# Four graph layers on one core: the first weights' product in column halves, and the last layer's third T inside the first maximum's turn

## What is computed

```
h = jnp.maximum(_layernorm(x, axis=-1), 0.0)          # layer 0
q = h @ Wq.T + bq;  k = h @ Wk.T + bk;  v = h @ Wv.T + bv
a = q @ k.T / sqrt(256) + adj + adj
x = x + softmax(a, axis=-1) @ v
...
h = jnp.maximum(_layernorm(x, axis=-1), 0.0)          # layer 3
g = h @ W
scores = where(adj + eye > 0, g @ U @ g.T, -inf)
att = softmax(scores, axis=-1)
x = x + (S * att) @ g                                 # S = adj + eye
```

## Time and profile before

| | |
|---|---|
| median of 3 runs | 401.05 us (400.98 to 401.45) |
| profiled execution | 400.99 us, its span 399.2 us |
| PE busy | 386.3 us, 97% of the span |
| DVE busy | 338.0 us, 85% |
| ACT busy | 251.9 us, 63% |
| POOL busy | 119.3 us, 30% |

### The profile page before, as it was taken

The page is one execution under the profiler, slowest core; times in us unless marked ns, Lnnn a source line. Parts: engine busy times, 40 slices in busy tenths (PEclk is TensorE's granted clock), DMA queues, the critical chain, the costliest instruction groups (busy, mean ns, idle before and its releaser), DMA issues. The chain is left out here.

```text
span 399.2 us, 7765 instructions
## 1 busy us (share of the span) xinstructions
PE 386.3 (97%) x2651; PEld 355.7 (89%) x2651; DVE 338.0 (85%) x772; ACT 251.9 (63%) x529; POOL 119.3 (30%) x131
## 2 busy tenths in 40 slices
PE   8999999999999999999999999999999899999894
PEld 6788888999899899999999889998988688989794
DVE  5898899899994857999999989766887988799894
ACT  2454699888785658785787992245242466257772
POOL 1290000000010424223041011051010499469982
PEclk9999999999999999999999999999999999999988
DMA  7995000000000001000000000000000000010011
GB/s 241 377 380 167 0 0 2 2 0 2 0 2 0 2 0 54 2 2 0 3 2 0 3 0 2 0 2 2 0 2 0 0 2 2 0 54 1 2 53 36
DMA packets 10318, 13.98 MB, mean 35 GB/s; under 512 B 660, under 2 KB 7208, under 8 KB 10280
## 3 DMA queue, kind: packets, MB, share of 16 engines
q1 hardware_dynamic: 9736, 12.96, 9.5%
q10 hardware_dynamic: 544, 0.52, 0.4%
HBM read 12.10 MB, written 1.39 MB: 34 GB/s over the span
## 5 line engine op out<-in xcount | busy, mean ns | idle before, releaser
L1611 PE MATMUL ps<-v_hi,p_hi 128*128 128x258 f32 (+3 forms) x242 | 64.0, 295 | 0.4 <-DVE x_sb L998 0.2
L397 POOL TENSOR_TENSOR mr_all<-mr_all,mhalf 128x4 f32<-128x4 f32 (+1 forms) x12 | 13.1, 1088 | 165.0 <-DVE mr_all L894 165.0
L1612 PE MATMUL ps<-v_lo,p_hi 128*128 128x258 f32 (+3 forms) x242 | 60.9, 281 | 0.0
L1611 PEld LDWEIGHTS ps<-v_hi,p_hi 128*128 128x128 f32 (+3 forms) x242 | 44.6, 184 | 2.2 <-issue 0.9
L1612 PEld LDWEIGHTS ps<-v_lo,p_hi 128*128 128x128 f32 (+3 forms) x242 | 44.7, 185 | 0.6
L1616 PE MATMUL ps<-v_hi,p_lo 128*128 128x258 f32 (+3 forms) x242 | 40.1, 284 | 1.1 <-DVE p_lo L1178 1.1
L980 DVE TENSOR_TENSOR s_sb<-s_sb,ps 128x512 f32<-128x512 f32 (+3 forms) x63 | 38.4, 611 | 0.8 <-PE ps L1598 0.7
L434 POOL TENSOR_TENSOR mid_lo<-adjT_sb,mid_hi 128x512 fp32r<-128x512 f32 (+2 forms) x16 | 20.9, 1306 | 49.7 <-ACT mid_hi L669 49.7
L1616 PEld LDWEIGHTS ps<-v_hi,p_lo 128*128 128x128 f32 (+3 forms) x242 | 32.5, 185 | 1.6 <-DVE p_lo L1178 1.6
L1903 PE MATMUL ps<-big_hi,p_lo 128*128 128x256 f32 (+3 forms) x121 | 32.7, 299 | 0.6 <-ACT p_lo L854 0.5
L1611 PE MATMUL ps<-big_hi,mid_hi 128*128 128x258 f32 (+3 forms) x121 | 31.8, 294 | 0.0
(11 more groups left out here) (251 smaller groups left out, 1218.3 us busy)
## 6 DMA issues: line engine op xcount, KB each, us to landing
adjT_sb<-in_adjT_dram SPq DMA_DIRECT2D x1, 2816.0 KB, 16.5
adjT_sb<-in_adjT_dram SPq DMA_DIRECT2D x3, 768.0 KB, 8.9
adjT_sb<-in_adjT_dram SPq DMA_DIRECT2D x1, 1815.0 KB, 20.9
out_dram<-x_sb SPq DMA_DIRECT2D x10, 128.0 KB
x_sb<-in_x_dram SPq DMA_DIRECT2D x2, 256.0 KB, 3.8
x_sb<-in_x_dram SPq DMA_DIRECT2D x1, 512.0 KB, 3.9
adjT_sb<-in_adjT_dram SPq DMA_DIRECT2D x1, 512.0 KB, 11.1
rows_sb<-in_rows_dram SPq DMA_DIRECT2D x1, 385.0 KB, 11.2
```

The costliest lines, as they stand in the source:

```text
L1611: pe.matmul(out_ap, left_[0][0:k, n % RING, mine], right_[0][0:k, j, 0:cols_], start=(j == 0), stop=False)
L1612: pe.matmul(out_ap, left_[0][0:k, n % RING, mine], right_[1][0:k, j, 0:cols_], start=False, stop=False)
```

## The change

**Beginning.** The product of the weights is made in column halves: `weight_half(m)` gives columns m*128 to m*128 + 127 of both row blocks, so that part m of T needs half m alone (before, a half was one row block, and each part needed both). Half 1 has a 129th column: ACT copies bk behind Wk (`wk_sb` is 257 wide now), and the product with Wq comes out with the half; the eight passes of `weight_column(6, ...)` go, and PE waits for that copy (`col_set`). z is (x + (-mean)) times the root, so for the first group POOL's second operation goes. One `idle` matmul is added ahead of the product, the one ahead of `weight_column(6, ...)` goes. `values(0)` stands ahead of the first score, `values(1)` between the score's halves. ACT and DVE follow that order; DVE splits `wb` and does the second group's statistics ahead of T's split, and `bqc` moves behind them.

**Layer 3.** `make_t(2, 1)` moves from step 9 to step 11, between `turn_max(0)` and `spread_max(0)`; `values(8)` goes behind `spread_max(0)`. On DVE the split of that T goes behind `shift(0)`, and the zeroing of `spare_mask` takes its old place at step 9. T's third group lies in banks 0 and 3 in place of 6 and 7; on ACT the first `w_hi` goes ahead of `values(10)` and waits for T's split.

```
-B0 = Banks([0, 1], [2, 3], [3, 7], [6, 5], [4, 5, 6, 7])
+B0 = Banks([0, 1], [2, 3], [7, 3], [6, 5], [4, 5, 6, 7])
-T3_BANKS = [[0, 1], [6, 7], [6, 7]]
+T3_BANKS = [[0, 1], [6, 7], [0, 3]]
...
+                if layer == gi == 0:
+                    ins.then_inc(ln, 1)
+                    return
...
-            for m in range(C):
-                act.wait_ge(gq_mm, m + 1)
-                split(0, wa_hi[:, m, 0:D], ps[:, 7 - 4 * m, m * D:(m + 1) * D], HALF_SCALE)
+            act.wait_ge(cols_in, 16)
+            act.activation(wk_sb[:, :, D:D + 1], bk_col.unsqueeze(2), ACT.Copy).then_inc(col_set, 1)
+            act.wait_ge(gq_mm, 1)
+            split(0, wa_hi[:, :, 0:P], half_product(0)[:, :, 0:P], HALF_SCALE)
             for b in range(4):
                 h_hi(b, 0)
+            act.wait_ge(gq_mm, 2)
+            act.activation(raw_b[:, :, D:D + 1], half_product(1)[:, :, P:P + 1], ACT.Copy, scale=HALF_SCALE).then_inc(col_set, 1)
+            split(0, wa_hi[:, :, P:D], half_product(1)[:, :, 0:P], HALF_SCALE)
...
+            t_hi_part(2, 1)
             values(8, 1)
-            for n in range(NT):
+            exp3(0)
+            values(9, 1)
+            exp3(1)
+            act.wait_ge(t_lo[1], 2 * NG)
+            w_hi(0)
+            values(10, 1)
+            for n in range(2, NT):
                 exp3(n)
-                if n < 2:
-                    values(n + 9, 1)
-                if n:
-                    w_hi(n - 1)
+                w_hi(n - 1)
...
-            dve.wait_ge(gq_mm, 1)
-            split_lo(0, wa_lo[:, 0, 0:D], ps[:, 7, 0:D], wa_hi[:, 0, 0:D], HALF_SCALE, 1)
             dve.wait_ge(ln, 1)
             for b in range(4):
-                dve.tensor_scalar(z_buf[:, b, :], x_sb[:, b, :], mr_all[:, b, 1:2], mr_all[:, b, 0:1], ALU.mult,
-                                  ALU.add).then_inc(zd, 1)
-            split_lo(0, wa_lo[:, 1, 0:D], ps[:, 3, D:2 * D], wa_hi[:, 1, 0:D], HALF_SCALE, 2)
+                dve.tensor_scalar(z_buf[:, b, :], x_sb[:, b, :], mr_all[:, b, 0:1], mr_all[:, b, 1:2], ALU.add,
+                                  ALU.mult).then_inc(zd, 1)
+            split_lo(0, wa_lo[:, :, 0:P], half_product(0)[:, :, 0:P], wa_hi[:, :, 0:P], HALF_SCALE, 1)
             for b in range(4):
                 h_lo(b, 0)
+            split_lo(0, wa_lo[:, :, P:D], half_product(1)[:, :, 0:P], wa_hi[:, :, P:D], HALF_SCALE, 2)
...
+            def weight_half(m):
+                n = P + m
+                for k in range(C):
+                    for c in range(C):
+                        ins = pe.matmul(half_product(m)[:, k, 0:n], wq_sb[:, c, k * P:(k + 1) * P], wk_sb[:, c, m * P:m * P + n],
+                                        start=(c == 0), stop=(c == C - 1))
+                ins.then_inc(gq_mm, 1)
...
                 for c in range(C):
+                    if a == 0 and n == 0 and c:
+                        values(1, 0)
                     pe.wait_ge(t_lo[a], 2 * gi + c + 1)
...
-                if s == 9:
-                    make_t(2, 1)
-                if s == 11:
-                    pe.wait_ge(t_lo[1], 2 * NG)
-                    turn_max(0, 1)
+                if s == 11:
+                    pe.wait_ge(t_lo[1], 2 * C)
+                    turn_max(0, 1)
+                    make_t(2, 1)
+                    spread_max(0, 1)
                     values(8, 1)
-                    spread_max(0, 1)
```

More of the change, by code:

```diff
@@ L901, in h_lo, with t_lo_part @@
                                          op1=ALU.subtract).then_inc(hlo, 1)
-            def t_lo_part(gi, a):
-                for m, bank in enumerate(T3_BANKS[gi] if a else B0.moved):
+            def t_lo_part(gi, a, parts=(0, 1)):
+                for m in parts:
+                    bank = (T3_BANKS[gi] if a else B0.moved)[m]
                     at_ = slice(gi * BANK, gi * BANK + CW[gi])
@@ L1501, in turn, with weight_product @@
                 ins.then_inc(zt, 1)
-            def weight_product(bank, lhsT, rhs, halves=range(C)):
-                for m in halves:
+            def weight_product(bank, lhsT, rhs):
+                for m in range(C):
                     for c in range(C):
@@ L1543, in values, with make_t @@
                 project(ps[0:rows(b), bank, 0:n], b, layer, (wb_hi, wb_lo), n).then_inc(v_mm[a], 1)
-            def make_t(gi, a):
+            def make_t(gi, a, parts=range(C)):
                 layer = 3 if a else 0
@@ L1554, in make_t @@
                 hT = hT3 if a else hT0
-                for m, bank in enumerate(T3_BANKS[gi] if a else B0.moved):
+                for m in parts:
+                    bank = (T3_BANKS[gi] if a else B0.moved)[m]
+                    if a == gi == 0:
+                        pe.wait_ge(wlo[0], m + 1)
                     wait(pe, t_lo[a], 2 * (gi - 1) + m + 1)
@@ L1661, in _ @@
                 score(s, 0)
-                if s == 0:
-                    pe.wait_ge(wlo[1], 1)
-                    pe.wait_ge(col_set, 1)
-                values(s, 0)
+                if s == 1:
+                    pe.wait_ge(col_set, 4)
+                if s > 1:
+                    values(s, 0)
                 if s == 6:
```

65 lines of the change are left out of this document (33 added, 32 removed).

## The result

The changed kernel takes 398.62 us (median of 9 runs, 398.40 to 399.11) where the kernel before takes 401.05 (9 runs, 400.73 to 404.35): a ratio of 0.9936 with a 95% interval of 0.9918 to 0.9954. It is faster by 2.43 us. The prediction had the sign, but its 399.9 and its range (399.1 to 401.1) lie above the result: the gain is more than twice the 1.1 us forecast. The profiled execution took 398.4 us, its span 396.6.

What follows compares the result with a forecast made beforehand. PE was taken to bound the steady part, with time to gain only at its waits and idle passes: 400.99 less 0.65 (beginning) and 0.45 (layer 3) gives 399.9 us. Own range 399.4 to 400.4, full range 399.1 to 401.1.

Steps and rivals of the forecast that it cites:

- z starts near 7.75: Beginning: with POOL's multiplication and DVE's split out of its way, z starts 0.8 us earlier than 8.54.
- The passes of 128 columns: Weights' product at the beginning: passes 0.12 us apart, like the turn's, so half 0 takes 1.0 us.
- The rival of halves as dear as before: Beginning: a 128-column pass costs what one of 256 does, the beginning gives 0.1, 400.4 to 400.5; chance 0.12.
- DVE's chain to T's split "is what is last": Beginning: DVE's chain, not PE, is last; T's split starts near 14.8, 0.55 us later than before, the score at 15.7.
- PE's own arrival: Beginning: PE reaches the first half of the score at 15.5 and waits 0.2 us there for DVE.
- From there on nothing waits: Beginning, from the score's first half: `values(1)` between the halves covers the second split (0.75); both are done at 18.0.
- The prediction's bound of 1.0: Beginning: upper bound of its gain, 1.0 us if PE meets no wait at all; 0.65 was taken.
- Layer 3: Late place of the change: T's 1.84 us on PE hide the reduction, first `shift` 0.9 earlier, first sum 0.45 earlier.
- The bound of 0.65: Layer 3: upper bound of its gain, 0.65 us if DVE's split overlaps better; 0.45 was taken.
- A fall of the clock at the beginning: Rival on the clock at the beginning, chance 0.10; part of it, 0.07, is slower than 401.85.
- DVE stays behind: Rival: DVE's room runs out; the beginning gives only 0.3 or layer 3 only 0.15, time 400.2; chance 0.12.
- more than forecast: Rival: nothing waits in either place, the beginning or layer 3, time 399.2; chance 0.08.

Runs made afterwards that it cites:

- the late zeroing: Changed kernel with DVE's zeroing of `spare_mask` moved from step 9 to behind the last operation of the running extreme: 398.39 us, then 398.16 against the changed kernel's 398.61.

## Why the prediction was wrong

- **z starts near 7.75**: 7.57, right; x had landed 0.16 earlier, by chance. The weights' product started at 6.64 and not at 7.05, as the clock had risen earlier, at 6.0; behind z that changed nothing. The passes of 128 columns: 9.28 to 10.17 for eight, 0.11 apart, right. The rival of halves as dear as before is refuted.
- **DVE's chain to T's split "is what is last", the step that failed.** The working put half 1 at 9.6 to 10.55, ACT's copy and split of it at 10.8 to 11.4, `wb_hi` to 12.05, the statistics at 12.7 and T's split at 14.8. Measured: half 1 at 9.28, `wb_hi` from 10.71 to 11.35, the statistics at 11.99, T's split at 13.92, 0.88 earlier, and what is last is PE. Of half 1's 0.3, z's own start is 0.18. ACT adds 0.4: the copy, the split and `wb_hi` start 0.07 and 0.27 apart, 0.34 in all, where the working had 0.6, near the sum of the durations (0.17 + 0.38), and the hand-over from half 1 was 0.1 shorter. The working took starts for DVE and durations for ACT. ACT's three operations in a row overlap by 0.10 and 0.11 us here (10.37 + 0.17 against 10.44, 10.44 + 0.38 against 10.71), and that alone is half of the 0.4. From the statistics on the working was nearly right, 1.93 against 2.1.
- **PE's own arrival, which then decided,** was costed at 15.5 and was 15.01: T started at 10.99 and not 11.4, for half 1's 0.3 and 0.1 less for half 1 and the bias column. So the 0.87 by which the turn of block 4 came before 18.0 is made of three parts: 0.2 that DVE's chain was not last (15.7 against PE's 15.5), 0.5 of PE's own arrival, and 0.18 behind it, 2.12 against 2.3, since half a score takes 0.70 and not 0.8. DVE's chain costed right would have given 17.8 and not 17.13: each term on PE was a little too dear as well.
- **"From there on nothing waits"** and the swap of `values` were right, and are worth 1.0 of the 1.5. The prediction's bound of 1.0, PE meeting no wait, was too low since it counted the waits and not what stood before them.
- **A term that was missing**: 0.57 between the places, 0.3 of it at 99 us. Some 0.4 is there in every trace and goes with the number of DVE's instructions; the rest is this pair of executions. Nothing in the diff tells it, but the wait put down to "issue" stood in the trace of before.
- **Layer 3**: the turn comes 3.47 - 2.06 = 1.41 earlier (forecast 1.4), the spread 0.88 (0.95), the first `shift` 0.94 (0.9). The first sum gives 0.58 and not 0.45, since from `shift` to first sum it is now 6.44 against 6.08, 0.36 more where the working had 0.45. Mechanism right, the term 0.13 too small. The bound of 0.65 was about all there was, as PE itself was done 0.15 before the first sum. The change kept a cost that was not needed, the zeroing at step 9, which the late zeroing takes away.
- **A fall of the clock at the beginning**, to which the forecast gives 0.10 (its 0.07 for slower than 401.85 comes from there): it did not come. In the changed kernel the granted clock reads 1.00 from 6 to 20 us, and half 1 goes on behind the turns at 0.11 a pass. That standstills of PE of 0.1 to 0.2 us bring the clock down, no run shows. But the clock mattered from the other side: how late it rises moved the old start, which the forecast had read from one trace as a fixed 0.25 a pass.
- **DVE stays behind**: no. Of the range, only "more than forecast" at 399.2 pointed the right way, and its chance of 0.08 took a trace with no wait at all for the best case. Of the 1.54 that the forecast lacks in this pair, 0.84 is the start, 0.57 the stretch between and 0.13 layer 3.
